# Adding an expert layer's rows into the output by accumulating scatters, in place of a scatter to scratch rows and a summing pass

## The reference, cut to what matters

```python
# per batch element: a 0/1 mask of the 10240 largest entries of adj
adj = (emb_s * emb_t) * (softmax(x) / sqrt(n)); adj[diagonal] = -inf
m = one at the top 10240 entries, zero elsewhere            # (4, 1024, 1024)
# a mixture of 8 experts on the mask's rows, two experts per row
scores = softmax(m @ G); value, indices = top_k(scores, 2)
gated = silu(m @ gate_w[e]) * (m @ up_w[e])
out = sum_e w[e] * (gated @ down_w[e] + (m @ lora_A[e]) @ lora_B[e])
return x + out                                              # float32 (4, 1024, 1024)
```

## Time and profile before

| what | us |
|---|---|
| median of 3 runs (lowest, highest) | 812.58 (808.84, 816.08) |
| span of the profiled execution | 807.6 |
| median of the runs less that span | 5.0 |
| PE / DVE / ACT / POOL busy in the span | 521.7 / 515.2 / 453.9 / 390.2 |

### The profile page before, as it was taken

How to read it: one execution, slowest core, us unless ns; L and a number is a source line. 1 busy time by engine, 2 the same in 40 slices (tenths; PEclk the granted TensorE clock), 3 DMA queues, 4 the chain that set the end, 5 groups by cost and what they waited for, 6 DMA issues and landing times.

```text
span 807.6 us, 14610 instructions
## 1 busy us (share of the span) xinstructions
PE 521.7 (65%) x4178; PEld 356.3 (44%) x4178; DVE 515.2 (64%) x1242; ACT 453.9 (56%) x655; POOL 390.2 (48%) x337
## 2 busy tenths in 40 slices
PE   0311287179878872787889817887888278888900
PEld 0300276066545542555546515554556155555500
DVE  5768889757597675765786776657773623232345
ACT  5687387749844574387445654883456145455500
POOL 8114200115375222577887125878872168768510
PEclk9855599579999995899999958997999779999965
DMA  9990160024323553478478834685579249858469
GB/s 313 359 265 0 58 256 27 13 65 157 111 78 126 200 223 121 131 246 288 155 246 265 351 113 145 230 292 173 192 259 372 79 147 311 270 189 279 179 252 382
DMA packets 80443, 159.93 MB, mean 198 GB/s; under 512 B 22889, under 2 KB 32105, under 8 KB 79856
## 3 DMA queue, kind: packets, MB, share of 16 engines
q1 hardware_dynamic: 59760, 108.60, 39.0%
q0 software_dynamic: 20608, 50.37, 17.9%
HBM read 107.53 MB, written 73.40 MB: 224 GB/s over the span
## 4 chain that ended last, share of the span: by engine, by line
DMA 25%; POOL 18%; issue 15%; DVE 14%; PE 13%; ACT 7%; DVEq 3%; SPq 3%; POOLq 1%; ACTq 0%
DMA out_dram<-piece 7%; DMA piece<-put_rows 7%; DMA put_rows<-y,where 5%; POOL piece L528 4%; POOL piece L531 4%; ACT mask L793 3%; PE pa L678 3%; DMA xg<-mask_rows,where 3%; POOL xg L511 3%; POOL put_rows L519 2%; DVE w L1169 2%; DMA w<-put_rows 2%; DVE mask L1063 2%; ACT y L850 2%; PE pb L665 2%
## 5 line engine op out<-in xcount | busy, mean ns | idle before, releaser
L678 PE MATMUL pa<-w,xt 128*128 x1472 | 198.7, 289 | 1.9 <-issue 1.8
L678 PEld LDWEIGHTS pa<-w,xt 128*128 128x128 f16 x1472 | 146.8, 100 | 58.2 <-issue 12.9
L850 ACT ACTIVATE y<-pc,where 128x512 f32<-128x512 f32 x184 | 124.1, 686 | 78.9 <-PE pc L704 58.7
L511 POOL DMA_INDIRECT xg<-mask_rows,where x92 | 98.8, 1074 | 125.6 <-DVEq L1331 95.2
L519 POOL DMA_INDIRECT put_rows<-y,where x92 | 92.5, 1005 | 134.1 <-ACT y L850 112.6
L1339 DVE SCALAR_TENSOR_TENSOR g_full<-pa,where,s_act 128x144 f32<-128x144 f32 x92 | 33.6, 365 | 185.2 <-ACT s_act L842 184.8
L837 ACT ACTIVATE xt<-pb 128x1024 f16<-128x1024 f16 x92 | 94.2, 1024 | 99.0 <-PE pb L665 96.3
L665 PE MATMUL pb<-ident,xg 128*128 128x128 f16 x736 | 62.1, 233 | 68.7 <-DMA xg<-mask_rows,where 47.8
L665 PEld LDWEIGHTS pb<-ident,xg 128*128 128x128 f16 x736 | 49.2, 105 | 79.7 <-DMA xg<-mask_rows,where 53.3
L842 ACT ACTIVATE s_act<-pa,small 128x128 f32<-128x128 f32 x92 | 33.8, 368 | 87.1 <-PE pa L678 87.1
L701 PE MATMUL pc<-wd,gt 128*128 x184 | 76.0, 413 | 5.1 <-ACT y L850 4.6
(11 more groups left out here) (208 smaller groups left out, 879.2 us busy)
## 6 DMA issues: line engine op xcount, KB each, us to landing
piece<-put_rows SPq DMA_DIRECT2D x96, 256.0 KB, 3.9
v<-in_x_dram SPq DMA_DIRECT2D x40, 512.0 KB, 9.0
piece<-in_x_dram SPq DMA_DIRECT2D x48, 256.0 KB, 2.9
out_dram<-piece SPq DMA_DIRECT2D x48, 256.0 KB
mask_rows<-mask SPq DMA_DIRECT2D x4, 2048.0 KB, 17.2
w<-put_rows SPq DMA_DIRECT2D x16, 512.0 KB, 9.5
w<-in_L_ffn_gate_w_dram SPq DMA_DIRECT2D x8, 512.0 KB, 10.2
w<-in_L_ffn_up_w_dram SPq DMA_DIRECT2D x8, 512.0 KB, 8.3
```

Of the source, the lines that this page charges most:

```text
L511: pool.indirect_dma_start(out=xg[:, g % NX, :], out_offset=None, in_=mask_rows[n % 2], in_offset=bass.IndirectOffsetOnAxis(ap=mask_row[n][ ...
L678: last = pe.matmul(l1[g % 2], xt[:, g % 2, t, :], w1[:, bass.ds(e, 1), t, k, :].rearrange("p o n -> p (o n)"), start=(t == 0 and k == 0), ...
L850: nc.scalar.activation(y[:, g % NY, half * HALF:(half + 1) * HALF], pc[:, half, :], ACT.Copy, scale=y_scale[n][:, i:i + 1]).then_inc(y_rea ...
```

## The change

`put_rows`, the pieces and the final sum go. Instead `out` itself is the target.

- `copy_x(n)` on SP copies x of image n from DRAM to DRAM into `out` (4 MB each): images 0 and 1 behind the weight loads and ahead of the first `move_mask`; image 2 behind `load_t(1)`, image 3 behind `load_t(2)`.
- `add_out(n, i, half)` on POOL takes the place of `put_out`: an indirect transfer that adds (`compute_op=ALU.add`) 128 half rows of 512 columns to rows of `out` seen as half rows. Two per tile. Each waits for its half of y and for the scatter of the same half of the tile before it to have landed (`added[half]`); the first of an image also waits for the copies.
- `store_y` waits, for each half, that this half of the tile two before it has been added.
- A slot without a pair no longer is skipped: it adds its y, which is zero, to a row of its own (the partition's number) in another image's part of `out` (`UNUSED_REGION`). So all 23 tiles of an image add 128 rows.
- `take_slots` on DVE makes the new row numbers with a few more small operations, two of them behind further drains.
- The last image's second load of x and DVE's final sums go. SP ends by waiting for all scatters.

```diff
-            def load_piece(n, j): ...
-            def store_piece(n, j): ...
+            def copy_x(n):
+                sp.dma_start(out[n], x[n]).then_inc(x_copied[n], 16)
...
+            copy_x(0)
+            copy_x(1)
             move_mask(0)
             sp.wait_ge(scores_ready, 1)
             load_t(1)
+            for n in range(1, B):
+                if n + 1 < B:
+                    copy_x(n + 1)
+                move_mask(n)
+                if n + 1 < B:
+                    sp.wait_ge(scores_ready, n + 1)
+                    load_t(n + 1)
+            for half in range(2):
+                sp.wait_ge(added[half], 16 * T * B)
...
-            def put_out(n, i):
+            def add_out(n, i, half):
                 g = tile(n, i)
-                pool.wait_ge(y_ready, 2 * (g + 1))
+                pool.wait_ge(y_ready, 2 * g + half + 1)
+                if i == 0 and half == 0:
+                    pool.wait_ge(x_copied[n], 16)
+                    pool.wait_ge(x_copied[UNUSED_REGION[n]], 16)
+                if g > 0:
+                    pool.wait_ge(added[half], 16 * g)
                 pool.indirect_dma_start(
-                    out=put_rows[n % 2], out_offset=bass.IndirectOffsetOnAxis(ap=put_row[n][:, i:i + 1], axis=0),
-                    in_=y[:, g % NY, :], in_offset=None,
-                    bounds_check=ROLES * S - 1, oob_is_err=False).then_inc(put[g % NY], 16)
+                    out=half_rows,
+                    out_offset=bass.IndirectOffsetOnAxis(ap=put_row[n][:, half, i:i + 1], axis=0),
+                    in_=y[:, g % NY, half * HALF:(half + 1) * HALF], in_offset=None,
+                    bounds_check=2 * B * S - 1, oob_is_err=True, compute_op=ALU.add).then_inc(added[half], 16)
-            def sum_piece(n, j): ...
...
                     if i >= 3:
-                        put_out(n, i - 3)
+                        add_out(n, i - 3, 0)
+                        add_out(n, i - 3, 1)
...
-                    if n > 0 and i in PIECE_AT:
-                        sum_piece(n - 1, PIECE_AT[i])
...
-                if g >= NY and half == 0:
-                    act.wait_ge(put[g % NY], 16 * (g // NY))
+                if g >= NY:
+                    act.wait_ge(added[half], 16 * (g - NY + 1))
...
+                V.tensor_scalar(unused_here, pair, 0.0, unused_row[:, n:n + 1], ALU.is_equal, ALU.mult)
...
-                V.tensor_copy(put_row[n], none_here)
-                V.tensor_tensor(mask_row[n], none_here, second_here, ALU.add)
+                V.tensor_tensor(none_here, none_here, second_here, ALU.add)
+                dve.drain()
+                V.tensor_copy(mask_row[n], none_here)
+                V.scalar_tensor_tensor(unused_here, none_here, float(n * S), unused_here, ALU.add, ALU.add)
+                dve.drain()
+                for half in range(2):
+                    V.tensor_scalar(put_row[n][:, half, :], unused_here, 2.0, float(half), ALU.mult, ALU.add)
                 dve.drain()
```

More of the change, by code:

```diff
@@ L28 @@
 EXPONENT = 0x7F800000
-SKIP = 4096.0
+SKIP = 8192.0
 AIM = 28.0
@@ L70, in build @@
     NX, NY = 3, 2
-    PIECES, NC = 2 * C, 2
     assert F == P and E * R == P and E == 8 and C == 8 and B == 4
@@ L99, in build @@
     MAX_AT = {(19, 2): 0, (20, 0): 1, (20, 1): 2, (20, 2): 3, (21, 0): 4, (21, 2): 5, (22, 0): 6, (22, 2): 7}
-    PIECE_AT = {**{j + 1: j for j in range(9)}, **{j + 4: j for j in range(9, PIECES)}}
-    PIECES_FIRST = 14
+    UNUSED_REGION = (1, 0, 1, 2)
+    assert len(UNUSED_REGION) == B
     with ExitStack() as ctx:
@@ L128, in build @@
         y = sb("y", [P, NY, H], F32)
-        piece = sb("piece", [P, NC, 3, HALF], F32)
+        spare = sb("spare", [P, 6 * HALF], F32)
         gr_parts = sb("gr_parts", [P, HT, PARTS, E], BF16)
@@ L137, in build @@
         slot_no = sb("slot_no", [P, P], F16)
-        where = sb("where", [P, 2, 5, T], F32)
+        where = sb("where", [P, 2, 6, T], F32)
         small = sb("small", [P, 352], F32)
@@ L148, in build @@
         raw_down = [wd[:, e, :, :].rearrange("p q h -> p (q h)").bitcast(F32) for e in range(E)]
-        spare = piece[:, :, :, :].rearrange("p i k h -> p (i k h)")
         raw_A = spare[:, 0:H]
@@ L201, in build @@
         tiles_below, tiles_to = temp(E), temp(E)
-        none_here, second_here = temp(T), temp(T)
+        none_here, second_here, unused_here = temp(T), temp(T), temp(T)
         tile_past = temp(T * E).rearrange("p (j e) -> p j e", j=T)
@@ L213, in build @@
         expert_no, tile_no, token_1 = cell(E), cell(T), cell(C)
+        slot_row, unused_row = cell(), cell(B)
         lower = cell(E * E).rearrange("p (a e) -> p a e", a=E)
@@ L238, in build @@
         mask_row = [table_of(n, 0, I32) for n in range(B)]
-        put_row = [table_of(n, 1, I32) for n in range(B)]
+        put_row = [where[:, n % 2, 4:6, :].bitcast(I32) for n in range(B)]
         g_scale = [table_of(n, 2) for n in range(B)]
         y_scale = [table_of(n, 3) for n in range(B)]
-        expert = [table_of(n, 4, I32) for n in range(B)]
+        expert = [table_of(n, 1, I32) for n in range(B)]
         pa = ps("pa", [P, 2, 512])
@@ L267, in build @@
         mask_rows = [nc.dram_tensor(f"mask_rows{i}", [S, H], F16, kind="Internal").ap() for i in range(2)]
-        put_rows = [nc.dram_tensor(f"put_rows{i}", [ROLES * S, H], F32, kind="Internal").ap() for i in range(2)]
         x_landed = [sem(f"x_landed{c}") for c in range(C)]
@@ L294, in build @@
         gathered = [sem(f"gathered{i}") for i in range(NX)]
[L295 to L301, removed]
+        added = [sem(f"added{half}") for half in range(2)]
+        x_copied = [sem(f"x_copied{n}") for n in range(B)]
         xt_turned, xt_ready, l1_done, silu_done = (
@@ L307, in build @@
         x_rows = x.rearrange("b (p c) h -> b p c h", c=C)
[L308 to L312, removed]
+        half_rows = out.rearrange("b s (k h) -> (b s k) h", k=2)
         side_rows = side.rearrange("b (p c) o -> b p (c o)", c=C)
@@ L381, in move_mask @@
                     load_x(n + 1)
-                else:
-                    for c in range(C):
-                        sp.dma_start(v[:, c, :], x_rows[n][:, c, :]).then_inc(last_x_landed[c], 16)
                 if n >= 2:
@@ L439, in _ @@
             nc.gpsimd.iota(token_1.bitcast(I32), pattern=[[1, C]], base=1, channel_multiplier=C)
+            nc.gpsimd.iota(slot_row.bitcast(I32), pattern=[[1, 1]], base=0, channel_multiplier=1)
             nc.gpsimd.iota(slot_int.bitcast(I32), pattern=[[1, P]], base=0, channel_multiplier=0)
@@ L447, in _ @@
                                     base=0, pattern=[[1, P]], channel_multiplier=-1)
-            for ints in (expert_no, tile_no, token_1):
+            for ints in (expert_no, tile_no, token_1, slot_row):
                 nc.gpsimd.tensor_copy(ints, ints.bitcast(I32))
             nc.gpsimd.tensor_copy(slot_no[:, :], slot_int.bitcast(I32))
+            pool.drain()
+            for n in range(B):
+                nc.gpsimd.tensor_scalar(unused_row[:, n:n + 1], slot_row,
+                                        float((UNUSED_REGION[n] - n) * S) - (SKIP - 1.0), None, ALU.add)
             pool.drain()
@@ L514, in gather @@
                     bounds_check=S - 1, oob_is_err=False).then_inc(gathered[g % NX], 16)
-            def put_out(n, i):
+            def add_out(n, i, half):
                 g = tile(n, i)
-                pool.wait_ge(y_ready, 2 * (g + 1))
-                pool.indirect_dma_start(
-                    out=put_rows[n % 2], out_offset=bass.IndirectOffsetOnAxis(ap=put_row[n][:, i:i + 1], axis=0),
-                    in_=y[:, g % NY, :], in_offset=None,
-                    bounds_check=ROLES * S - 1, oob_is_err=False).then_inc(put[g % NY], 16)
[L524 to L532, removed]
+                pool.wait_ge(y_ready, 2 * g + half + 1)
[4 more added lines that the diff above has]
+                    pool.wait_ge(added[half], 16 * g)
+                pool.indirect_dma_start(
+                    out=half_rows,
+                    out_offset=bass.IndirectOffsetOnAxis(ap=put_row[n][:, half, i:i + 1], axis=0),
+                    in_=y[:, g % NY, half * HALF:(half + 1) * HALF], in_offset=None,
+                    bounds_check=2 * B * S - 1, oob_is_err=True, compute_op=ALU.add).then_inc(added[half], 16)
             for n in range(B):
@@ L538, in _ @@
                     gather(n, i)
-                if n >= 2:
-                    pool.wait_ge(summed_piece, PIECES * (n - 1))
                 for i in range(T):
@@ L551, in _ @@
                             below_third(n + 1, q)
-                    if n > 0 and i in PIECE_AT:
-                        sum_piece(n - 1, PIECE_AT[i])
                 for i in range(T - 3, T):
-                    put_out(n, i)
+                    add_out(n, i, 0)
+                    add_out(n, i, 1)
         @block.tensor
@@ L1438, in _ @@
                     route(n + 1)
[L1441 to L1448, removed]
```

## The result

The changed kernel takes 879.97 us (median of 4 runs, 878.05 to 883.61) against 813.33 us before in the same comparison: a ratio of 1.080, 95% interval 1.076 to 1.085. It is slower by 66.6 us, where a gain of some 14 had been forecast. What came about is the pace of the second rival, the chain that paces every tile; it had been priced at 857. Whether for that rival's reason is taken up further down.

A forecast was written before the change was run, and what follows sets the result against it. The prediction took the chain of half scatters, each waiting for the last to land, as the new pacer. Its terms summed to -14.3 us: 812.6 - 14.3 = 798, range 772 to 895.

The forecast's parts named there:

- the second rival: Scatter chain paces every tile, reads of source and destination then write in turn: L 5.15, period 5.89, 857 us; chance 0.37.
- L: Time from start to landing of an adding scatter of 128 x 2 KB on POOL, taken as 4.3 us.
- the other half: Within L, 0.3 us added because the tile's other half scatter shares the DMA engines for part of the time.
- DMA_INDIRECT itself well over 1.0 us: Sign of being wrong: POOL's adding scatter instruction taking well over the 1.0 us assumed.
- The restart: POOL's time from a landing's semaphore to the start of the next scatter's transfer, 0.74 us per tile.
- the period: Time per tile of the scatter chain, L plus restart: 5.04 us, under the 5.29 of image 0 before.
- The copy of image 3: Copy of image 3's x meets image 0's last adds and image 1's first gathers: +2 us (0 to 5).
- +7 in images 0 and 1: Chain in traffic: half scatters beside the next x load and mask store hold up y and ACT's queue; +7 us each.
- the 34 us of the final sum: At the end of image 3 these go whole, the slower chain giving 8 back: -26.2 us.
- landings beside the x load of about 10: A half scatter beside the load of the next x and the mask's store should take about 10 us.
- two copies hidden in the set-up at +1: Copies of images 0 and 1 lie hidden in idle DMA time during set-up: +1 us, up to 45 without that cover.
- tiles over 5.5 us apart: Sign of being wrong: tiles 5.5 us apart or more, POOL waiting for `added` in every tile, PE idle between.

The follow-up runs named there:

- e8: Changed kernel with slots without a pair given a row past the end and skipped, no zeros added: 860.55 us, 19.4 less than the changed kernel's 879.97.
- e6: Changed kernel with only the first 512 columns of each tile added, the second half made but not scattered: 845.7 us in a single run.
- e3: Changed kernel with its scatters made plain, without the addition, halves, order and waits unchanged: 775.17 us in a single run.
- e5: Changed kernel with one adding scatter of 1024 columns per tile in place of two of 512: 945.47 us, 1.158 of the kernel before.
- e1: Changed kernel with four y buffers in place of two: 863.99 us, 1.060 of the kernel before.

## Why the prediction was wrong

**The step that failed is the size of L**, and within it the fixed part. It was built as 3.4 for a gather (2.2 empty and 1.2 of reads) + 0.65 (half a scatter's writes) + 0.3 (the other half), taken as 4.3. Measured: 2.7 empty [e8], 4.8 for a half alone [e6], 4.9 with the other half. So data and other half together were put at 2.15 and measured 2.2, which is luck: the data alone takes 2.1 and not 1.85, the other half 0.1 and not 0.3. What is missing is the fixed part, 2.7 and not 2.2: that of the plain transfers was taken, and the adding one's instruction takes 1.6 and not 1.0. The prediction had listed "DMA_INDIRECT itself well over 1.0 us" as what would show it wrong, and priced it at nothing.

By the sum's own terms L = 4.9 alone turns the forecast round, from -14 to about +23 (835). The restart adds to that: 0.84 and not 0.74, on every link. With the period measured, 5.87 and not 5.04 is +18 over image 3's 22 tiles, +1 at the end for the landing, and 22 x (5.87 - 5.29) = 12.8, so +38, for images 0 to 2. That makes 855. The second rival's 857 at a period of 5.89 was the same sum, but its reason was another: it had reads one after the other and then the writes, 3.05 us of data behind an empty transfer of 2.1. The data takes 2.1 and the empty transfer 2.7, so its nearness is luck too.

**The copy of image 3** had +2, hidden by "image 0's last adds, which nobody waits for". Somebody did: the y behind them, and in ACT's order the exponentials behind the y. It costs 12.4. A transfer's cover has to be followed through every engine's queue behind it: not only who waits for the scatter, but what stands behind the one that waits. With the +10 that this is more than assumed, the sum is 865.

**The other 15 us** are not taken apart. With four buffers, so that y hardly waits in ACT's queue, 16 go, some 6 of them the same as the copy's. But the forecast had already given +7 in images 0 and 1 for just that queue, beside the load of the next x. So between 5 and 15 us stay without a name.

What held: the 34 us of the final sum went, and the chain took most of them back; landings beside the x load of about 10; two copies hidden in the set-up at +1, with the first add of image 0 at 185.9, ahead of the 187 that would have shown them late; PE's pace of 4.19 as what the kernel could do, which e3 reaches. The signs of being wrong came too: tiles over 5.5 us apart, and y waiting for landings 95 times, not only beside the x load. e8 prices a point that the forecast had named and carried inside its full links: the zero rows of the empty tiles, 19 us.

The Trainium skill, Collectives: The Full Stack, section "The bandwidth ceiling: the fold count and why AG ≠ RS ≠ AR", has an add in the DMA engines cost only its second read. By the gather's row that made 2.4 us of data for a half; 4.8 less 2.7 is 2.1. The runs show it more closely by what another 2 KB a row adds: 1.4 us with the addition (6.2 less 4.8), 0.7 without (3.4 less 2.7 [e3]). That is twice, so the runs agree with the page on the rate. They show two parts that the section does not name: 0.6 of instruction, and some 0.7 (2.1 less 1.4, an estimate) that 128 added rows take whatever their length.

## What to carry to other kernels

A chain of dependent DMAs costs its landing plus the restart for every link, however little it moves, and that has to be set against the pace of the slowest engine with a margin: here 5.9 a tile where 5.3 had been the pace makes, with image 3's share, 57 of the 82 us between forecast and run. Price the instruction and the landing of an operation that the trace does not show apart, fixed part and data part, and let the fixed part be uncertain too. And where an engine in order waits for a landing, ask what unrelated work stands behind it.

## What the runs showed of the hardware

- An indirect scatter with addition takes POOL 1.55 to 1.59 us for 128 rows, of 2 KB or 4 KB, against 0.99 to 1.01 without; empty, it lands after 2.7 against 2.1 us.
- Behind an empty transfer's 2.7 it takes 2.1 us more for 128 x 2 KB [e6] and 3.5 for 128 x 4 KB [e5], against 0.6 [e3] and 1.3 behind the 2.1 of a plain scatter.
- A copy of 4 MB from DRAM to DRAM lands after 15.5 to 17.6 us (27.6 where it follows another at once), and a small scatter that is issued behind it lands after 16 to 18 us, when the copy does.
- In this profile a wait for two semaphores that are set free by one event was put down to the engine that ended last, ACT, though taking 149 of ACT's 171 us of waiting away [e1] moved the pace by 3%.
